# A layer norm, selective scan and router kernel: the router's dot products and three step-size sums on TensorE, one input product fewer on GpSimd

## The reference

```python
x = x + s6(layernorm(x))                 # selective scan
x = x + mod(layernorm(x))                # attention and feed-forward on the chosen tokens

def s6(x):                               # d = 512 channels, n = 16 states
    xp = x @ x_proj_w.T                  # 96 columns: 64 rank, 16 B, 16 C
    delta = softplus(d_rank @ dt_proj_w.T + dt_proj_b)
    h[t] = exp(delta[t] * A) * h[t-1] + delta[t] * B[t] * x[t]     # per channel and state
    y[t] = sum_n h[t] * C[t] + x[t] * D

def mod(x):
    weights = (x @ router_w)[..., 0] + router_b[0]   # the router: one dot product a token
    # the 128 largest of a batch; threshold, attention and MLP on 127 of them,
    # out = processed * weight, other tokens keep x * (1 - selected)
```

## Time and profile before

| | |
|---|---|
| device time, median of 3 runs | 4456.08 us (4455.1 to 4457.46) |
| profiled execution, its own time | 4463.26 us |
| its span | 4461.5 us |
| busy: VectorE | 3768.9 us (84%) |
| busy: GpSimd | 3363.5 us (75%) |
| busy: TensorE matmul, weight load | 3066.8 us (69%), 1408.3 us (32%) |
| busy: ScalarE | 2861.0 us (64%) |
| scans (VectorE, L821) | 1024 of 2270 ns |
| products `ch` (GpSimd, L955) | 1024 of 2358 ns |

### The profile page before, as it was taken

How to read it: one execution, slowest core, us unless ns; L and a number is a source line. 1 busy time by engine, 2 the same in 40 slices (tenths; PEclk the granted TensorE clock), 3 DMA queues, 4 the chain that set the end, 5 groups by cost and what they waited for, 6 DMA issues and landing times. The chain is left out here.

```text
span 4461.5 us, 61468 instructions
## 1 busy us (share of the span) xinstructions
PE 3066.8 (69%) x17574; PEld 1408.3 (32%) x17574; DVE 3768.9 (84%) x3027; ACT 2861.0 (64%) x4425; POOL 3363.5 (75%) x1716
## 2 busy tenths in 40 slices
PE   4667665766676666665665756666664289999997
PEld 1222232322232222222232323222222145555553
DVE  2999999999999999999999999999998754555552
ACT  5777777777778687868777777777774223332221
POOL 3999999999999999999999999999998100000010
PEclk7767676767766676667676767676775589999998
DMA  4454546463646455554545464636453300000000
GB/s 102 104 136 121 148 114 158 96 170 87 171 101 156 114 144 130 127 136 122 134 123 135 124 152 105 164 84 180 92 146 76 144 22 20 19 19 19 19 19 8
DMA packets 198219, 472.94 MB, mean 106 GB/s; under 512 B 60688, under 2 KB 61200, under 8 KB 197088
## 3 DMA queue, kind: packets, MB, share of 16 engines
q1 hardware_dynamic: 177136, 452.11, 40.3%
q0 software_dynamic: 20736, 16.88, 1.4%
HBM read 126.83 MB, written 73.43 MB: 45 GB/s over the span
## 5 line engine op out<-in xcount | busy, mean ns | idle before, releaser
L955 POOL TENSOR_TENSOR ch<-hid,cmat 128x1024 f32<-128x1024 f32 x1024 | 2385.4, 2358 | 92.7 <-DVE hid L821 76.4
L821 DVE TENSOR_TENSOR_SCAN hid<-place,inp 128x1024 f32<-128x1024 f32 x1024 | 2266.1, 2270 | 105.4 <-ACT place L671 87.3
L671 ACT ACTIVATE place<-delr,a_neg 128x1024 f32<-128x1024 f32 x1024 | 1126.8, 1111 | 293.6 <-DVE hid L821 190.2
L444 PE MATMUL ps_y<-ch,nsum 128*32 128x256 f32 x8192 | 856.5, 517 | 424.3 <-POOL ch L955 423.4
L810 DVE TENSOR_TENSOR inp<-place,bmat 128x1024 f32<-128x1024 f32 x816 | 941.6, 1211 | 64.2 <-ACT place L677 63.4
L455 PE MATMUL ps_y<-ident,ysb 128*128 128x128 f32 x1024 | 319.2, 408 | 599.0 <-ACT ysb L684 580.0
L444 PEld LDWEIGHTS ps_y<-ch,nsum 128*32 128x32 f32 x8192 | 254.6, 137 | 1025.6 <-POOL ch L955 753.2
L917 POOL TENSOR_TENSOR inp<-dxr,bmat 128x1024 f32<-128x1024 f32 x208 | 490.2, 2357 | 0.0
L455 PEld LDWEIGHTS ps_y<-ident,ysb 128*128 128x128 f32 x1024 | 230.5, 278 | 807.9 <-ACT ysb L684 759.1
L1216 POOL DMA_INDIRECT out_rows<-row,idx_out x16 | 41.1, 2571 | 532.3 <-issue 298.4
L439 PE MATMUL ps_y<-xhT,dskip 128*32 128x256 f32 x2048 | 260.8, 600 | 134.2 <-ACT xr L691 134.2
(11 more groups left out here) (176 smaller groups left out, 4202.8 us busy)
## 6 DMA issues: line engine op xcount, KB each, us to landing
dxr<-dxT SPq DMA_DIRECT2D x1024, 128.0 KB, 2.4
delr<-delT SPq DMA_DIRECT2D x1024, 128.0 KB, 2.4
xr<-in_x SPq DMA_DIRECT2D x32, 1024.0 KB, 6.6
bmat<-b_and_c SPq DMA_DIRECT2D x256, 128.0 KB, 3.4
cmat<-b_and_c SPq DMA_DIRECT2D x256, 128.0 KB, 3.1
x_rows<-xr SPq DMA_DIRECT2D x16, 2048.0 KB, 7.7
out_rows<-xr SPq DMA_DIRECT2D x32, 1024.0 KB, 5.1
w<-in_w SPq DMA_DIRECT2D x2, 4096.0 KB, 24.4
```

Source lines behind the costliest of these rows:

```text
L444: last = pe.matmul(ps_y[q * CH:(q + 1) * CH, 0:2 * P], nsum[:], ch[:, g, q * 2 * P:(q + 1) * 2 * P], start=False, stop=(g == GROUPS - 1))
L671: nc.scalar.activation(place[:, PLACE[par, c, g], :], delr[:, c % 2, :], ACT.Exp, scale=a_neg[:, i:i + 1])\
L821: nc.vector.tensor_tensor_scan(hid[:, g, :], place[:, PLACE[par, c, g], :], inp[:, g, :], 0.0, ALU.mult, ALU.add).then_inc(hid_ready, 1)
L955: nc.gpsimd.tensor_tensor(ch[:, g, :], hid[:, g, :], cmat[:, g, :], ALU.mult).then_inc(ch_ready, 1)
```

## The change

- **Router.** The dot product of the second norm with the router's weights w is taken apart: (x1 - mean) w / std, with x1 = x + y. The part with x comes out of the projection: its weight matrix gets 32 more columns that all hold w, and `router_x` turns that row to tokens by 8 products of one column (behind `xhT`, so it is of the normalised x, and `scale_route_x` on GpSimd scales it back by three small instructions, with std from one more in `ln1_finish`). The part with y comes from `ysb`, which now keeps all 16 chunks: `router_y` makes 2 products of 4 columns for each chunk, in five pieces (`ROUTE_Y`), and `copy_router_y` copies them out. `route` joins both with five small instructions. VectorE's `router` and ScalarE's `copy_rw` are gone.
- **Step size.** Block 1's terms are summed by `add_terms` and `copy_step`, no longer by GpSimd's steps 0 to 2. Its places are (14, 3), (15, 1) and (15, 2), with the copies at (15, 1) and (0, 0). Block 2's z moves from chunk 15 to chunk 0, its logs from chunk 0 to chunk 1, its sums from chunks 0 to 2 into 2 to 4. Block 3's stay.
- **Products in place.** GpSimd writes hid x C over `hid`. `ch` is gone (its memory goes to `ysb`), TensorE sums `hid`, and the scan waits for `ch_summed` (TensorE) in place of `ch_ready` (GpSimd).
- **Own inputs.** `OWN_AT` has 12 chunks: 4, 13 and 14 leave it and 15 comes in.
- **First norm's sums** start at (5, 0) in place of (5, 3), and wait for each half of x by itself.

```diff
-SUMS1 = {(5, 3): range(0, 3), (6, 0): range(3, 6), (6, 1): range(6, 9), (6, 2): range(9, 13), (6, 3): range(13, 17)}
+SUMS1 = {(5, 0): range(0, 1), (5, 1): range(1, 2), (5, 2): range(2, 3), (5, 3): range(3, 5), (6, 0): range(5, 7),
+         (6, 1): range(7, 10), (6, 2): range(10, 13), (6, 3): range(13, 17)}
-Z = (12, 13, 15)
+Z = (12, 13, 16)
-         (14, 3): (1, 1, 0), (15, 0): (1, 1, 1), (15, 2): (1, 1, 2), (1, 0): (0, 1, 3),
-         (2, 3): (0, 2, 3), (7, 3): (0, 3, 3)}
-ADD_TERMS = {(2, 0): ((0, 2), (0, 3), (1, 1)), (2, 1): ((1, 1), (1, 2), (2, 1)),
+DELTA = {(13, 0): (1, 0, 0), (13, 1): (1, 0, 1), (13, 2): (1, 0, 2), (13, 3): (1, 0, 3), (0, 1): (0, 1, 3),
+         (4, 1): (0, 2, 3), (7, 3): (0, 3, 3)}
+ADD_TERMS = {(1, 0): ((14, 3), (14, 3), (15, 1)), (1, 1): ((15, 1), (15, 2), (0, 0)),
+             (2, 0): ((2, 3), (2, 3), (3, 1)), (2, 1): ((3, 1), (3, 2), (4, 0)),
              (3, 0): ((5, 2), (5, 3), (6, 1)), (3, 1): ((6, 1), (6, 2), (7, 1))}
-       (0, 0): (0, 2, (0,)), (0, 1): (0, 2, (1,)), (0, 2): (0, 2, (2,)),
+       (1, 0): (0, 2, (0,)), (1, 1): (0, 2, (1,)), (1, 2): (0, 2, (2,)),
-RW_COPY = (2, 1)
-ROUTER = (2, 3)
+ROUTE_Y = {(0, 3): range(0, 5), (1, 1): range(5, 8), (1, 2): range(8, 10), (1, 3): range(10, 15), (2, 1): range(15, 16)}
+COPY_ROUTE_Y = (2, 3)
+ROUTE_X = (13, 3)
+COPY_ROUTE_X = (14, 1)
+SCALE_ROUTE_X = (15, 1)
-OWN_AT = tuple(range(1, 14))
+OWN_AT = (1, 2, 3, 5, 6, 7, 8, 9, 10, 11, 12, 15)
...
+            def router_x(b):
+                aux_free(b, ("route_x",))
+                for t in range(TC):
+                    last = pe.matmul(aux[:, t:t + 1], xpT[R + 2 * N:P, t * P:(t + 1) * P],
+                                     ident[R + 2 * N:P, R + 2 * N:R + 2 * N + 1], start=True, stop=True)
+                last.then_inc(aux_full, 1)
+            def router_y(b, cs, emptied):
+                if 0 in cs:
+                    pe.wait_ge(aux_emptied, emptied)
+                for c in cs:
+                    for t in range(2):
+                        last = pe.matmul(aux[:, 4 * t:4 * t + 4], ysb[:, c, t * P:(t + 1) * P], rw_chunk[:, c, :],
+                                         start=(c == 0 and t == 0), stop=(c == CHUNKS - 1 and t == 1))
+                last.then_inc(route_y_full, 1)
...
 # scan, VectorE
-                    dve.wait_ge(ch_ready, tile(b, c, g) - GROUPS + 1)
+                    dve.wait_ge(ch_summed, tile(b, c, g) - GROUPS + 1)
 # product, GpSimd
-                        if has(b, 1) or c > 0:
-                            pool.wait_ge(ch_summed, tile(b, c, g) - GROUPS + 1)
-                        nc.gpsimd.tensor_tensor(ch[:, g, :], hid[:, g, :], cmat[:, g, :],
+                        nc.gpsimd.tensor_tensor(hid[:, g, :], hid[:, g, :], cmat[:, g, :],
...
 # route, GpSimd
+                pool.wait_ge(ln2, b * LN2 + LN2)
+                pool.wait_ge(route_y_copied, b + 1)
+                nc.gpsimd.tensor_tensor(route_t[:, 0, :], m2[:, 1, :], rw_sum[:].to_broadcast([P, TC]), ALU.mult)
+                nc.gpsimd.tensor_tensor(route_t[:, 1, :], route_y[:], route_in[:, par, 0, :], ALU.add)
+                nc.gpsimd.tensor_tensor(route_t[:, 2, :], route_t[:, 1, :], route_t[:, 0, :], ALU.add)
+                nc.gpsimd.tensor_tensor(route_t[:, 1, :], route_t[:, 2, :], r2[:, 4, :], ALU.mult)
+                nc.gpsimd.tensor_tensor(wcol[:, bass.ds(b * TC, TC)], route_t[:, 1, :], rb[:].to_broadcast([P, TC]), ALU.add)
...
 # start, ScalarE, batch 0
-            for k in range(3):
-                if k == 2:
-                    copy_dx(0, 0, 0)
-                    for g in range(2):
-                        exp_decay(0, 0, 0, g)
+            for k in range(2):
                 for h in range(2):
                     z_half(0, k, h)
                 exp_log(0, k)
+            copy_router_x(0)
+            copy_dx(0, 0, 0)
+            for g in range(2):
+                exp_decay(0, 0, 0, g)
+            copy_step(0, 1, 0)
...
 # end, ScalarE: behind the last copy_x1, ahead of the last norm's sums
-            copy_rw(last, nb_run * NUSE)
+            copy_router_y(last)
             ln2_sums(last, 1, range(17))
 # end, TensorE: behind the last turn_y
+            for cs in ROUTE_Y.values():
+                router_y(nb_run - 1, cs, nb_run * NUSE)
```

More of the change, by code:

```diff
@@ L423, in add_terms @@
                     aux_free(b, ("s", k, h))
+                    if (k, h) == (2, 0) and has(b, 1):
+                        pe.wait_ge(route_y_copied, b)
                     pe.wait_ge(z_act, b * KD * ZACT + k * ZACT + ZACT)
@@ L463, in _ @@
                 project(0, 0, h)
-            for k in range(3):
+            for k in range(2):
                 for h in range(2):
                     step_size(0, k, h)
+            router_x(0)
+            for h in range(2):
+                for first in (True, False):
+                    add_terms(0, 1, h, first)
+            step_size(0, 2, 0)
             pe.wait_ge(dskip_ready, KD)
@@ L613, in ln1_sums @@
             def ln1_sums(b, par, steps):
+                for h in range(2):
+                    if 4 * h in steps:
+                        act.wait_ge(x_in[par][h], (b - par) * 8 + 16)
                 if 0 in steps:
-                    for h in range(2):
-                        act.wait_ge(x_in[par][h], (b - par) * 8 + 16)
                     if has(b, 1):
                         act.wait_ge(ln1, b * LN1)
+                        act.wait_ge(route_in_step, b * 3)
                 sums(b, par, steps, 0, m1, ln1_act)
@@ L683, in copy_y @@
                     act.wait_ge(yt_ready, b * CHUNKS + c)
-                nc.scalar.activation(ysb[:], ps_y[:, 0:2 * P], ACT.Copy).then_inc(ysb_ready, 1)
+                if c in ROUTE_READ and has(b, 1):
+                    act.wait_ge(route_y_full, (b - 1) * len(ROUTE_Y) + ROUTE_READ[c])
+                nc.scalar.activation(ysb[:, c, :], ps_y[:, 0:2 * P], ACT.Copy).then_inc(ysb_ready, 1)
             def copy_x1(b, par, c):
@@ L729, in beside @@
                     z_half(b, 3, 1)
-                if at in LOG and not LOG[at][0] and (LOG[at][1] == 3 or has(b, 1)):
+                if at in LOG and not LOG[at][0] and LOG[at][1] in (2, 3):
                     exp_log(b, *LOG[at][1:])
                 for (k, h), when in ADD_TERMS.items():
-                    if when[2] == at:
-                        copy_step(b, k, h)
+                    if when[2] == at and not (ahead(k, at) and is_last(b)):
+                        copy_step(b + ahead(k, at), k, h)
                 if has(b, 1):
@@ L851, in body @@
                         scan(b, par, c, g)
-                    if has(b, 1) and c in ROUTER:
-                        router(b - 1, other, ROUTER.index(c))
                     for g in range(GROUPS):
@@ L864, in _ @@
             batches(dve, body)
-            last = nb_run - 1
-            for h in range(2):
-                router(last, 1, h)
             dve.wait_ge(wt_ready, 1)
@@ L967, in body @@
                         if (c, g) == ROUTED and has(b, 1):
-                            route(b - 1)
+                            route(b - 1, 1 - par)
+                        if (c, g) == SCALE_ROUTE_X and not final:
+                            scale_route_x(b + 1, 1 - par)
                     if c + 1 in OWN_AT:
```

171 lines of the change are left out of this document (111 added, 60 removed).

## The result

The change makes the kernel slower: 4477.27 us (median of 5 runs, 4473.8 to 4480.41) against 4456.08 (4452.09 to 4460.87) beside it. The ratio is 1.0045, 95% interval 1.0033 to 1.0058. The forecast was 4428. The profiled execution of the kernel after took 4474.66 us (span 4472.9).

What follows compares the result with a forecast made beforehand. Scan phase bound by VectorE and GpSimd at once. Per batch, -5.0 us of work and stalls up from 7.0 to 9.6 make -2.4; over 15 batches -36, end +8, total -28: median 4428, range 4355 to 4485.

Steps and rivals of the forecast that it cites:

- VectorE -5.0, GpSimd -7.4: Own work per batch, without stalls: VectorE falls 5.0 us to 198.4, GpSimd 7.4 us from 205 to 198.
- The new wait: 0: The scan's wait for TensorE's sum instead of GpSimd's product: taken as 0 us a batch, bounds 0 and 4.4.
- GpSimd's own input for chunk 15: 0.7: This new input ends about 0.7 us behind the start of the scan that reads it: 0.7 us stall a batch.
- The edge, 1.4 + 2.0, and the loop's edge, 1.0: Block 1's terms stall the batch's edge 1.4 and 2.0 us; the loop's edge adds 1.0 on the mean.
- rival B: TensorE's clock rises at the batch's edge, four terms take 4.1 us, stalls 5.3 a batch: 4362 us; chance 0.23.
- Chunks 1 and 2, 2.5: ScalarE's added log passes beside the second norm's steps stall 1.2 us in chunk 1, 1.3 in chunk 2.
- Chunk 4, 1.0: Block 2's copy of (2, 1) at (4, 0) delays two exps by 0 to 3 us, taken as 1.0.
- Chunk 7, 1.0: Chunk 7's stall falls from 1.9 to 1.0 us, as two first-norm sums move into chunk 5.
- The end, +8: Once, behind the last turn_y: 32 router products at 0.25 us each and GpSimd's longer chain add 8 us.
- Total -28: Whole kernel: -2.4 us a batch over 15 batches, -36, plus 8 at the end: 28 us faster.
- Rival A: TensorE-ScalarE-VectorE chain at the batch's edge takes more than the router gave, terms 8.3 us: 4491, up to 4544; chance 0.21.
- Rival C: Time taken off VectorE and GpSimd is not on the path; stalls rise by just 5 us: 4464 us; chance 0.16.

Runs made afterwards that it cites:

- experiment 11: Kernel before with VectorE's router products over 8 of 512 channels, all instructions and waits in place: 4407.16 us, ratio 0.9880.
- experiment 2: Kernel before with only the new wait: GpSimd writes hid*C over hid, the scan waits for TensorE's sum: 4455.96 us, ratio 1.0003.
- experiment 1: Kernel after with one of router_x's eight products left in place, every wait kept: 4441.47 us, ratio 0.9971.
- experiment 4: Kernel after with router_x's eight products in three pieces behind chunk 14's first three sums, their copy at (14, 3): 4468.14 us, ratio 1.0025.
- experiment 9: Kernel after with the loop written out, router_x in two pieces at (14, 0) and (14, 1), last router_y copy behind the last sums: 4416.04 us, ratio 0.9896.
- experiment 15: Kernel after with its loop, router_x in two pieces at (14, 0) and (14, 1), last router_y copy behind the sums: 4457.77 us, ratio 0.9997.
- experiment 13: Kernel after with one product in each of router_y's five pieces instead of 32 in all, waits and copies kept: 4443.30 us, ratio 0.9971.
- experiment 12: Kernel after with block 2's log passes moved from (1, 0), (1, 1), (1, 2) to (1, 2), (2, 1), (2, 2): 4503.57 us, ratio 1.0090.
- Experiment 8: Kernel after with ScalarE's last copy of router_y behind the last norm's sums instead of ahead of them: 4468.22 us, ratio 1.0019.
- Experiment 10: Kernel after, with the loop, one of router_x's eight products kept and the last router_y copy behind the sums: 4434.69 us, ratio 0.9944.
- experiment 5: Kernel after with the loop over pairs of batches written out, same work and order: 4457.47 us, ratio 0.9989.
- experiment 6: Kernel before with the loop over pairs of batches written out in the same way: 4440.16 us, ratio 0.9949.

## Why the prediction was wrong, step by step

- *VectorE -5.0, GpSimd -7.4*: right in the main. VectorE's busy time is 199.5 us a batch against the 198.4 forecast, GpSimd's 196.3 against 198. VectorE's router was on the path (experiment 11).
- *The new wait: 0*: right (experiment 2).
- *GpSimd's own input for chunk 15: 0.7.* This was the only stall forecast near chunk 14, and **here the prediction failed**: its sum counts "the router's 32 products" and has no term for `router_x`'s eight at (13, 3), ahead of `turn_y(13)`. Chunk 14's stall is 3.4 us, 2.7 more than forecast, which is 41 us over 15 batches. With seven of the eight products gone it is 0.5. The net effect of removing them is less, 33 us, since chunk 15 takes some back.
- *The edge, 1.4 + 2.0, and the loop's edge, 1.0*: measured some 1.0 together in the kernel after. The four terms took 3.5 us, not 6.2. That is the condition of rival B, and it goes with the place of the very products that were left out of the sum: with those gone or moved the terms took 4.5 to 5.7 us (experiments 1, 4, 9 and 15). In experiment 1 the forecast's stall of 1.4 measured 0.8 in odd batches and, with the loop's jump, 3.5 in even ones.
- *Chunks 1 and 2, 2.5*: measured 5.0. A `router_y` product was taken at 0.25 us and takes 0.43 at the low clock; experiment 13 gives 1.7 us a batch for them, 0.7 of it in these two chunks. The rest of the excess was not singled out; experiment 12 shows that ScalarE's log passes are part of chunk 1's stall.
- *Chunk 4, 1.0*: measured 0.1. *Chunk 7, 1.0*: chunks 6 and 7 have 3.3 together. The prediction read 1.9 there before; chunk 7's mean stall was 2.4. No experiment was made on this.
- *The end, +8*: mis-sized, measured +13.7. The 32 products took 13.65 us, 0.43 each, at a granted clock of 0.50 throughout; 0.25 was the price at the high one. Experiment 8 gives 12.8 of it back.
- *Stalls of 7.0 before*: its own rows give 211.4 - 203.4 = 8.0, and the mean of batches 1 to 14 is 7.8.
- *Total -28*: the stalls of a batch are 13.1 us, not 9.6, so a batch is 0.3 us longer and not 2.4 shorter. Over 15 batches that is 41 us, and the end adds 6: nearly all of the 49 between forecast and result. Experiment 10, with `router_x`'s term and the end's cost taken out, comes to 4431 beside the forecast's 4428, but that rests on luck: its end costs nothing where the forecast had 8 us, and its stalls are 11.3 us a batch where the forecast had 9.6. In the kernel after the edge's terms were 3.4 too high and chunks 1, 2, 6 and 7 together 4.8 too low.
- *Rival A* has the right sign and nearly the time (4491), and the stalls passed its 4.5 us (13.1 against 7.8 is 5.3 more). But they did so at another place, and its own condition, terms of 8.3 us, did not occur. *Rival C*'s sum, stalls up by 5 us, was nearly met as well, though its reason, that VectorE's time was not on the path, is ruled out by experiment 11.

## What to carry to other kernels

Cost every instruction that a change puts on an engine that works in order, small ones too. Look above all at those between the last piece of a chain and what the next engine waits for: seven products of one column cost 33 us here, while making the router on VectorE thin was worth 53. The same products one place later, behind the next chunk's first sums, cost nothing in that chunk; but look at what such a move meets one chunk on. Before trusting a loop, look at what its jump back exposes; writing it out was worth 23 to 45 us here.

## What had not been expected of the hardware

- A product of few columns with a new block of weights costs the same with one column as with four: `router_y`'s with 4 columns 0.43 us at the low clock (32 in 13.65), `router_x`'s with one column 0.44. At the high clock ten of 4 columns took 2.40 us, 0.24 each. The rows agree with the Trainium skill, TensorE: Matmul & The Clock Gate, "LDWEIGHTS (loading the stationary operand)", that a load costs by its 128 columns and not by its rows: `router_x`'s block has 32 rows and costs as much as one of 128. The page's length for it, 128 / 1.2 = 107 ns, is near the 120 ns from record to record at the high clock (two records a product) and half of the 213 ns at the low one.
- The jump back of a loop leaves engines without a releaser: TensorE 3.0 to 3.6 us before and 6.9 to 7.4 after, VectorE 0 to 4.4 over all these kernels. That these are fetches of instructions is argued from the queues' packets and from experiments 5, 6 and 9, not seen by itself. Why VectorE's part is 0 to 0.7 us in the kernel after and 2.8 to 4.4 in experiments 1, 4 and 15, with the same list on VectorE, stays open.
- The clock of the same four terms depended on where other small products stood. Eight of them behind chunk 13's last sum gave 3.5 us for the terms, in every batch. One product gave 5.1 to 5.6, though TensorE had less to do, and eight among chunk 14's sums gave 4.5 to 5.7 (experiments 4, 9 and 15), in experiment 9 with TensorE busy 6.00 of the 6 us ahead. What decides it stays open.
